# Layer transitions by halves of 512 tokens in an eight-layer gated transformer kernel

## The reference

```python
x = x + tanh(g_xattn[0]) * mixture_by_token_id(layernorm(x), ctx)     # layer 0
x = x + tanh(g_ffn[0])   * moe_32_and_16(layernorm(x))                # layer 1
x = x + tanh(g_xattn[1]) * quantised_attention(layernorm(x), ctx)     # layer 2
x = x + tanh(g_ffn[1])   * moe_48_kept_with_capacity(layernorm(x))    # layer 3
x = x + tanh(g_xattn[2]) * rope_attention_with_adapter(layernorm(x))  # layer 4
x = x + tanh(g_ffn[2])   * moe_2(layernorm(x))                        # layer 5
x = x + tanh(g_xattn[3]) * fp8_product(layernorm(x), ctx)             # layer 6
x = x + tanh(g_ffn[3])   * moe_8_and_shared(layernorm(x))             # layer 7
```

## Time and profile before

| | us |
|---|---|
| median of 3 runs | 1687.19 |
| profiled run | 1686.27 |
| its span | 1684.5 |
| TensorE busy | 1440.2 (85%) |
| VectorE busy | 1301.4 (77%) |
| ScalarE busy | 758.2 (45%) |
| GpSimd busy | 927.4 (55%) |
| mean granted TensorE clock | 0.804 |

### The profile page before, as it was taken

How to read it: one execution, slowest core, us unless ns; L and a number is a source line. 1 busy time by engine, 2 the same in 40 slices (tenths; PEclk the granted TensorE clock), 3 DMA queues, 4 the chain that set the end, 5 groups by cost and what they waited for, 6 DMA issues and landing times.

```text
span 1684.5 us, 31230 instructions
## 1 busy us (share of the span) xinstructions
PE 1440.2 (85%) x11436; PEld 854.1 (51%) x11436; DVE 1301.4 (77%) x2348; ACT 758.2 (45%) x1438; POOL 927.4 (55%) x861
## 2 busy tenths in 40 slices
PE   4688999999768998779999997578778898995698
PEld 2454555556423232645555555355555565563365
DVE  7857777777689998757777775888878876667885
ACT  4332222222258998322222223478878873232232
POOL 5535666666010140016666661599999993875072
PEclk9989999999855555789999998755555558997799
DMA  5201111111049999201111111388878861111010
GB/s 201 72 26 38 50 53 47 47 47 47 10 77 179 178 178 179 82 10 47 47 47 47 47 47 41 54 141 143 142 144 137 140 125 44 57 48 47 1 39 26
DMA packets 325104, 131.77 MB, mean 78 GB/s; under 512 B 308096, under 2 KB 308608, under 8 KB 324096
## 3 DMA queue, kind: packets, MB, share of 16 engines
q1 hardware_dynamic: 323840, 125.54, 35.9%
q10 hardware_dynamic: 1152, 4.74, 0.8%
HBM read 53.69 MB, written 1.05 MB: 32 GB/s over the span
## 4 chain that ended last, share of the span: by engine, by line
PE 55%; DVE 24%; POOL 13%; issue 3%; ACT 3%; DMA 2%; SPq 1%; POOLq 0%; DVEq 0%; ACTq 0%
PE s_all L708 40%; PE bank L708 8%; DVE small L1730 7%; POOL c_hi L628 4%; POOL c_lo L628 3%; PE s_all L792 2%; DVE xn L1414 2%; POOL c_hi L626 2%; POOL c_lo L626 2%; PE s_all L963 2%; DVE stats L1403 1%; DVE small L1733 1%; PE s_all L718 1%; DVE ffbuf L1575 1%; DVE x L1591 1%
## 5 line engine op out<-in xcount | busy, mean ns | idle before, releaser
L500 POOL TENSOR_TENSOR w_hi<-w_in,ws_col 128x768 f16<-128x768 f32 (+1 forms) x112 | 161.9, 1445 | 493.7 <-PE bank L708 476.9
L1546 DVE TENSOR_TENSOR hid_lo<-ffbuf,hid_hi 128x512 f16<-128x512 f32 x152 | 274.5, 1806 | 107.1 <-ACT hid_hi L1182 107.1
L1182 ACT ACTIVATE hid_hi<-ffbuf 128x512 f16<-128x512 f32 x152 | 95.7, 630 | 463.7 <-DVE ffbuf L1544 463.7
L708 PE MATMUL s_all<-xt_hi,w_hi 128*128 128x512 f16 x864 | 259.3, 382 | 19.5 <-DVE ffbuf L1544 8.0
L501 POOL TENSOR_SCALAR w_in<-w_in 128x768 f32<-128x768 f32 (+1 forms) x112 | 273.9, 2445 | 0.0
L708 PE MATMUL s_all<-xt_lo,w_hi 128*128 128x512 f16 x864 | 259.0, 381 | 0.0
L708 PE MATMUL s_all<-xt_hi,w_lo 128*128 128x512 f16 x864 | 258.8, 381 | 0.0
L504 POOL TENSOR_TENSOR w_lo<-w_in,w_hi 128x768 f16<-128x768 f32 (+1 forms) x112 | 184.8, 1650 | 9.3
L1730 DVE TENSOR_REDUCE small<-s_all 128x1 f32<-128x1024 f32 x128 | 155.5, 1215 | 13.2 <-PE s_all L963 13.2
L1273 ACT ACTIVATE ag<-s_all,small 128x1024 int16<-128x1024 f32 x128 | 154.1, 1204 | 19.6 <-DVE small L1733 9.6
L963 PE MATMUL s_all<-ag 32*128 32x512 f16 x256 | 131.4, 616 | 8.2 <-ACT ag L1273 3.7
(11 more groups left out here) (323 smaller groups left out, 2910.6 us busy)
## 6 DMA issues: line engine op xcount, KB each, us to landing
w_in<-in_w_blocks SPq DMA_DIRECT2D x112, 384.0 KB, 3.0
region<-in_w_attn SPq DMA_DIRECT2D x4, 512.0 KB, 10.6
sel<-in_k_sel ACTq DMA_DIRECT2D x1, 1280.0 KB, 6.9
sel<-in_k_sel ACTq DMA_DIRECT2D x1, 1152.0 KB, 5.6
ag<-ag SPq DMA_TRANSPOSE x66, 3.3
x<-in_x_in SPq DMA_DIRECT2D x1, 1024.0 KB, 4.8
region<-in_ctxt SPq DMA_DIRECT2D x1, 1024.0 KB, 9.4
ffbuf<-in_mask ACTq DMA_DIRECT2D x1, 1024.0 KB, 4.7
```

The source lines that it names most:

```text
L500: nc.gpsimd.tensor_tensor(hi, w, ws_col[:, 0:1].broadcast_to([P, used]), ALU.mult).then_inc(s_g, 1)
L708: m = nc.tensor.matmul(outp, lhs, rhs, start=(first and n == 0), stop=(last and n == len(steps) - 1), skip_group_check=True)
L1182: nc.scalar.activation(hid_hi[:, h, :], hid[:, h, :], ACT.Copy).then_inc(s_hh, 1)
L1546: nc.vector.tensor_tensor(hid_lo[:, h, :], hid[:, h, :], hid_hi[:, h, :], ALU.subtract).then_inc(s_hl, 1)
```

## The change

Each transition works by halves. `norm` becomes `norm(l, h)`, called behind the statistics of half h, with four tiles each; the square root runs once for each half. `transpose_xn` becomes `transpose_half(l, h)`, with bank 2h + k for feature half k. VectorE forms half 0's low parts after it has updated half 1 of x and ahead of half 1's statistics; half 1's low parts stay at the start of the layer. ScalarE's order is root of half 0, copies of half 0, root of half 1, copies of half 1, and only then tanh (layer 0) and the loads (layers 1 and 3). In layers 0, 5 and 7 TensorE does `gate_up(0)` between the two halves, then `gate_up(1)`, then the router. The router's first two parts on VectorE move from units 0 and 1 to unit 1, and ScalarE's exponential from unit 0 to unit 1. In the other layers TensorE still waits for both halves.

```diff
+            def transpose_half(l, h):
                 n = XT_ORDER.index(l)
+                pe.wait_ge(ln_xn, l * NT + 4 * h + 4)
+                for k in range(KT):
                     for j in range(4):
+                        m = nc.tensor.transpose(bank[2 * h + k][:, j * P:(j + 1) * P],
                                                 xn[:, 4 * h + j, k * P:(k + 1) * P], ident[:, :])
                     m.then_inc(xt_ps, 1)
+            def half_ready(l, h):
+                pe.wait_ge(xt_l, 4 * XT_ORDER.index(l) + 2 * h + 2)
...
+                transpose_half(l, 0)
+                half_ready(l, 0)
                 gate_up(0)
+                transpose_half(l, 1)
+                half_ready(l, 1)
+                gate_up(1)
                 if l in ROUTER:
                     router(l)
-                gate_up(1)
...
-                if l in XT_ORDER:
+                if l in XT_ORDER and l not in EXPERTS:
                     transpose_xn(l)
```

On ScalarE:

```diff
-                    if n == 0 and l in ROUTER:
+                    if n == 1 and l in ROUTER:
                         router(l)
...
             for l in range(NLAYERS):
-                norm(l)
+                norm(l, 0)
+                if l in XT_ORDER:
+                    transpose_half(l, 0)
+                norm(l, 1)
+                if l in XT_ORDER:
+                    transpose_half(l, 1)
                 if l == 0:
                     act.wait_ge(s_first, 16 * FIRST_LOADS)
                     nc.scalar.activation(g_tanh[:, :], g_raw[:, :], ACT.Tanh).then_inc(s_setup_act, 1)
...
-                if l in XT_ORDER:
-                    transpose_xn(l)
```

On VectorE:

```diff
+            def norm(l, h):
+                tiles = range(4 * h, 4 * h + 4)
+                for i in tiles:
                     m = nc.vector.bn_aggr(moments[:, i, :], stats[:, i, :])
                 m.then_inc(ln_var, 1)
+                dve.wait_ge(ln_std, 2 * l + h + 1)
+                link(nc.vector.reciprocal(rstd[:, 4 * h:4 * h + 4], std[:, 4 * h:4 * h + 4]))
+                for i in tiles:
                     nc.vector.tensor_scalar(xn[:, i, :], x[:, i, :], moments[:, i, 0:1], rstd[:, i:i + 1],
                                             ALU.subtract, ALU.mult).then_inc(ln_xn, 1)
...
                     link(m)
-                    if l + 1 < LAYERS:
-                        measure(l + 1, 4 * h, 4 * h + 4)
+                    if h == 1 and l + 1 in XT_ORDER:
+                        transpose_half(l + 1, 0)
+                    measure(l + 1, 4 * h, 4 * h + 4)
+                    norm(l + 1, h)
...
-                    if l in ROUTER and n == 0:
+                    if l in ROUTER and n == 1:
                         router(l, 1)
-                    if l in ROUTER and n in (1, 2):
-                        router(l, n + 1)
+                        router(l, 2)
+                    if l in ROUTER and n == 2:
+                        router(l, 3)
...
+                    if b == 3:
+                        transpose_half(l + 1, 0)
                     measure(l + 1, 2 * b, 2 * b + 2)
+                    if b % 2:
+                        norm(l + 1, b // 2)
...
-            measure(0, 0, NT)
+            for h in range(2):
+                measure(0, 4 * h, 4 * h + 4)
+                norm(0, h)
+            transpose_half(0, 0)
             for l in range(NLAYERS):
-                norm(l)
                 if l in XT_ORDER:
-                    transpose_xn(l)
+                    transpose_half(l, 1)
```

More of the change, by code:

```diff
@@ L486, in _ @@
             weight_blocks(attn4_it, RUN_BLOCKS // RING)
[L487 removed]
+            sp.wait_ge(ln_var, 2 * LAYERS + 1)
             sp.dma_start(out, x[:, :, :]).then_inc(s_out, 16)
@@ L1147, in _, with transpose_half @@
         def _(act):
[L1148 to L1152, removed]
+            def norm(l, h):
+                act.wait_ge(ln_var, 2 * l + h + 1)
+                nc.scalar.activation(std[:, 4 * h:4 * h + 4], moments[:, 4 * h:4 * h + 4, 1], ACT.Sqrt, bias=eps[:, :]
+                                     ).then_inc(ln_std, 1)
+            def transpose_half(l, h):
                 n = XT_ORDER.index(l)
-                for b in range(4):
-                    act.wait_ge(xt_ps, 4 * n + b + 1)
-                    nc.scalar.activation(xt_hi[:, b // 2, (b % 2) * HALF:(b % 2 + 1) * HALF], bank[b][:, :],
+                for k in range(KT):
+                    act.wait_ge(xt_ps, 4 * n + 2 * h + k + 1)
+                    nc.scalar.activation(xt_hi[:, k, h * HALF:(h + 1) * HALF], bank[2 * h + k][:, :],
                                          ACT.Copy, scale=XS).then_inc(xt_h, 1)
@@ L1403, in measure, with norm, transpose_half @@
                     m = nc.vector.bn_stats(stats[:, i, :], x[:, i, :])
[L1404 to L1408, removed]
+                link(m)
+            def norm(l, h):
+                tiles = range(4 * h, 4 * h + 4)
+                for i in tiles:
                     m = nc.vector.bn_aggr(moments[:, i, :], stats[:, i, :])
                 m.then_inc(ln_var, 1)
-                dve.wait_ge(ln_std, l + 1)
-                link(nc.vector.reciprocal(rstd[:, :], std[:, :]))
-                for i in range(NT):
+                dve.wait_ge(ln_std, 2 * l + h + 1)
+                link(nc.vector.reciprocal(rstd[:, 4 * h:4 * h + 4], std[:, 4 * h:4 * h + 4]))
+                for i in tiles:
                     nc.vector.tensor_scalar(xn[:, i, :], x[:, i, :], moments[:, i, 0:1], rstd[:, i:i + 1],
                                             ALU.subtract, ALU.mult).then_inc(ln_xn, 1)
-            def transpose_xn(l):
+            def transpose_half(l, h):
                 n = XT_ORDER.index(l)
[L1419 to L1423, removed]
+                for k in range(KT):
+                    c = slice(h * HALF, (h + 1) * HALF)
+                    dve.wait_ge(xt_h, 4 * n + 2 * h + k + 1)
+                    nc.vector.scalar_tensor_tensor(out=xt_lo[:, k, c], in0=bank[2 * h + k][:, :], scalar=XS,
+                                                   in1=xt_hi[:, k, c], op0=ALU.mult, op1=ALU.subtract
                                                    ).then_inc(xt_l, 1)
@@ L1926, in fp8_gemm @@
                         link(m)
+                    if h == 1:
+                        transpose_half(7, 0)
                     measure(7, 4 * h, 4 * h + 4)
+                    norm(7, h)
             nc.vector.memset(zeros16[:, :], 0.0)
@@ L1958, in _ @@
                     fp8_gemm()
-            nc.vector.memset(small[:, 7, 0:1], 0.0).then_inc(ln_var, LAYERS + 1 - NLAYERS)
+            nc.vector.memset(small[:, 7, 0:1], 0.0).then_inc(ln_var, 1)
 NLAYERS = 8
```

10 lines of the change are left out of this document (4 added, 6 removed).

## The result

The changed kernel has a median of 1700.37 us (1699.14 to 1701.91, 4 runs) against 1688.87 (1686.88 to 1690.6, 4 runs): ratio 1.0076, 95% interval 1.0059 to 1.0094. It is slower by about 12 us (11.5 by the medians). The profiled run took 1701.29 with a span of 1699.5, 15.0 more than the span of before, 1684.5. The forecast was +8.9 us and 1696.1.

What follows compares the result with a forecast made beforehand. VectorE was taken to set a transition's length, with a tail of TensorE, ScalarE and VectorE behind it. The terms sum to +8.9 us, a span of 1693.4 and a run of 1695.2; the median lies 0.9 above, 1696.1; range 1688.5 to 1703.

Steps and rivals of the forecast that it cites:

- Plain transition: Layers 1 to 2 and 3 to 4: VectorE's longer chain, less a shorter tail, costs +1.7 us each.
- the term of the low parts: Plain transition: two low parts moved ahead of half 1's statistics cost 1.38 us, and waiting for copies about 0.5.
- Layer 2 to 3: Tail +1.3 us; loads reordered behind all copies on ScalarE let VectorE read the logits +3.0 us later in all.
- Layer 4 to 5: Half 0's gate product goes between the halves, so SiLU and the hidden product come earlier: -2.6 us.
- Layer 0 to 1: GpSimd's two-operand instructions hold up norm tiles of both halves: +3.0 us.
- Start of layer 0: Gate product 2.8 us early, but tanh and table loads stand behind both halves' copies, ahead of SiLU: +1.6 us.
- 5 to 6: No transposes; one more square-root round trip, and half 0's norm meets GpSimd: +0.9 us.
- 6 to 7: Half 0's product leads by 5.8 us but runs at 1.2 GHz, half 1's transposes queueing behind it: -0.4 us.
- A: Rival: early gate products of layers 0, 5 and 7 keep their leads to the third product; 1683.6 us, chance 0.07.
- B: Rival: GpSimd's instructions miss the norms and the loads land in time; no change, 1687.5 us, chance 0.13.
- C: Rival: all hold-ups hit and the clock stays low in layer 5; +18.5, 1705.7 us, chance 0.08.
- D: Rival: ScalarE table switches in layers 0 and 5 cost the skill's doubled price, 4.1 us more; 1700.2 us, chance 0.02.

Runs made afterwards that it cites:

- e2: Changed kernel with half 0's two low parts behind half 1's norm on VectorE, into layers 1 to 4; span 1689.1 us.
- e1: Changed kernel with the selector loads and layer 3's four small loads moved to behind half 0's copies on ScalarE; span 1699.2 us.
- e9b: e7 with the norm adding 1 instead of 2 to its semaphores; 1679.12 us, ratio 0.9945 to the kernel before.
- e10b: Kernel before the change plus extra identity transposes around the transposes of layers 1 to 5 and behind those of 7; median 1681.30 us, ratio 0.9955.
- e3: Changed kernel with half 0's SiLU ahead of half 1's copies, and its hidden product ahead of half 1's low parts, in layers 0, 5, 7; span 1697.7 us.
- e5: Changed kernel with extra identity transposes, into a bank nobody reads, where TensorE waits in a transition; span 1681.0 us.
- e4: Changed kernel with GpSimd waiting for layer 1's whole norm before splitting layer 1's first weights; span 1694.3 us.
- e7: Changed kernel with eight-tile norm everywhere, adding 2 to semaphores; in layers 0, 5, 7 half 0's product stays early, behind all transposes; span 1684.0 us.

## Why the prediction was right, and where it was off

The direction, the range (1688.5 to 1703) and the main mechanism hold: a step put earlier on VectorE pushes back everything behind it. The signs named in advance came too: half 0's low parts ahead of half 1's statistics, the cast ended by a load, layer 5's product right behind half 0's low parts. The number is 4.3 us short by the median; most terms were too low, and the gain of layer 5 did not come. Step by step:

- **Plain transition.** First product +1.88 for the forecast 1.7; from 3 to 4 it is +1.3. e2 confirms the term of the low parts (1.92 measured; 1.38 + 0.5). What the sum had no term for is the clock behind it, 0.8 from 1 to 2 and about 1.1 from 3 to 4 (the stage jumps by 2.4 there; the low level lasts 5.0 us behind the first product against 2.9). I had the fall and the return of the clock in the trace of before and priced neither, as both kernels have them.
- **Layer 2 to 3.** The wait for the load is there as described (716.81, ended by the DMA). At the logits the changed kernel is 2.5 later than it was ahead of the transition, for the forecast +3.0: the load cost 1.3 of it for 1.7, and the tail 1.2 for 1.3 (e1). The line is +3.9 by two stretches that the sum didn't have: 0.7 at the end of layer 2, ahead of the transition, where e9b and e10b with the norm of eight tiles are 0.7 and 0.6 later too, so it belongs to the trace of before; and 0.7 between the logits and layer 3's steady units. How much of the load's 1.3 reaches the units stays open (0.3 by e1, with its longer slow stretch).
- **Layer 4 to 5.** This step failed, forecast -2.6. First, I took the product at the full clock; it ran at 1.2 GHz (1419.52 to 1424.5) and held half 1's transposes, whose tiles were ready at 1422.5, until 1424.49. The price for that case, -0.6, stood as the bound and is near the measured -0.25. Second, SiLU was the wrong end of the chain (e3): what the layer waits for is half 1's product. At the full clock (e5) the start of layer 5 gains 2.2; but the kernel before gains 2.5 there from extra transposes alone (e10b), so that gain is the clock's and not shown to be the early half's.
- **Layer 0 to 1.** Mechanism right, +3.9 for +3.0: half 0's norm took 3.98 for the 3.7 that I followed, and half 1's 4.51 for 4.0; e4 shows that GpSimd was the cause of both. That the sizes fit so well is in part luck: with the same norms in the same place e2 has 4.04 and 2.39, e3 2.77 and 4.35, e5 2.80 and 4.92, as GpSimd's instructions happen to lie.
- **Start of layer 0.** +2.15 for +1.6. Tanh and SiLU's table stood in line (loads at 21.91 and 23.43, SiLU at 24.73); e3 gives 1.5 back.
- **5 to 6 and 6 to 7.** +0.77 for +0.9 and -0.56 for -0.4, the product at the low level as taken.
- **Rivals.** A falls by e3: even with ScalarE out of the way the leads are not kept. From 6 to 7 extra transposes give 1.6 more (e5, -2.2), and e9b has -2.0 with neither them nor a split. B didn't come: both norms of layer 1 were held up and the load was waited for. C's low clock in layer 5 came, the rest of it did not. D: tanh follows its table load by 0.02 (21.91 + 1.28, tanh at 23.21). The Trainium skill (ScalarE: Activation LUTs, What ACT_TABLE_LOAD costs) has a drain of 1.38 behind a load; no row here shows one.

## What to carry to other kernels

Splitting a transition so that one engine can start early is worth something only if what the next stage waits for comes earlier; here that was half 1, and every step of half 0 put ahead of it was a loss, unless the engine would have been idle in that place. A pause of TensorE costs twice, in the pause and at half speed behind it, so price a longer or a split pause with the slow work that follows; filling it with idle transposes gave more here than the reordering did. An engine that has time (GpSimd) is best kept out of the critical stretch of one that has none.

## What the runs showed of the hardware

- An instruction that adds 2 to a semaphore instead of 1 moved a wait on ScalarE onto the table load ahead of the square root: 1.28 of load and 0.02 of gap between aggregation and root (455.01, 456.31). Without it (e9b) the kernel is 5.1 us shorter than e7, part of which is how GpSimd fell on one norm.
- The same eight norm tiles took 2.67, 6.29 and 8.81 us from 0 to 1, by how GpSimd's instructions fell on them; a tile of 0.40 lasted 1.80 beside an instruction of 1.64 on GpSimd, while low parts beside such instructions kept their 0.69.
- With the same code, a stretch at 1.2 GHz lasted 13.7 us in one execution and 17.1 in another (changed kernel and e1, from 3 to 4), for 1.1 us of time.
- Eight transposes of 128 x 128 in float32 take 1.09 us at 2.4 GHz and 1.97 at 1.2 GHz.
